# Cross attention scores as two 64-row tiles side by side, in a ring of three PSUM banks

## What is computed

```python
q, k, v = proj(query, Wq, SQ), proj(key, Wk, SKV), proj(value, Wv, SKV)   # 16 heads of 8
scores = jnp.einsum('bhqd,bhkd->bhqk', q, k) / np.sqrt(HEAD_DIM)
scores = scores + attention_bias[:, None, None, :]
probs = jax.nn.softmax(scores, axis=-1)
out = jnp.einsum('bhqk,bhkd->bhqd', probs, v)
return out.transpose(0, 2, 1, 3).reshape(B, SQ, EMBED) @ Wo.T
```

## Time and profile before

| | us |
|---|---|
| runs (median, lowest, highest) | 475.95, 474.44, 659.19 |
| the profiled execution | 473.19 |
| its span, first to last instruction | 471.4 |
| PE busy | 423.8 |
| DVE, ACT, POOL busy | 345.6, 319.2, 298.4 |

### The profile page before, as it was taken

How to read it: one execution, slowest core, us unless ns; L and a number is a source line. 1 busy time by engine, 2 the same in 40 slices (tenths; PEclk the granted TensorE clock), 3 DMA queues, 4 the chain that set the end, 5 groups by cost and what they waited for, 6 DMA issues and landing times.

```text
span 471.4 us, 16299 instructions
## 1 busy us (share of the span) xinstructions
PE 423.8 (90%) x6928; PEld 291.3 (62%) x6928; DVE 345.6 (73%) x544; ACT 319.2 (68%) x675; POOL 298.4 (63%) x250
## 2 busy tenths in 40 slices
PE   3338988988999999999999999999999899989995
PEld 2125766356676776776767767667666575555674
DVE  6363437987777877778777787778777654868796
ACT  6424632466887788788787878887877686564563
POOL 7879479689686685685775855957776461443100
PEclk9756976599999999999999999999999999999999
DMA  6476338646958858569469497495263000000000
GB/s 156 151 136 138 115 83 228 134 151 136 198 156 131 184 157 142 167 119 196 134 109 211 133 142 131 122 129 152 75 170 80 4 3 1 1 0 1 25 1 18
DMA packets 78112, 53.30 MB, mean 113 GB/s; under 512 B 62952, under 2 KB 69208, under 8 KB 78040
## 3 DMA queue, kind: packets, MB, share of 16 engines
q1 hardware_dynamic: 76216, 50.91, 48.5%
q0 software_dynamic: 1280, 0.87, 0.6%
q10 hardware_dynamic: 544, 0.48, 0.3%
HBM read 17.05 MB, written 0.46 MB: 37 GB/s over the span
## 4 chain that ended last, share of the span: by engine, by line
PE 72%; DVE 12%; ACT 5%; POOL 5%; issue 3%; DMA 2%; ACTq 1%; DVEq 0%; POOLq 0%
PE ps L1047 18%; PE ps L872 13%; PE ps L1023 6%; PE ps L375 4%; PE ps L377 4%; PE ps L376 4%; PE ps L875 4%; DVE mx L1625 3%; PE ps L1170 3%; PE ps L800 3%; PE ps L801 2%; PE ps L803 2%; DVE mself L1485 2%; PE ps L905 2%; PE ps L882 2%
## 5 line engine op out<-in xcount | busy, mean ns | idle before, releaser
L1625 DVE TENSOR_REDUCE mx<-ps 120x2 f32<-120x1000 f32 x192 | 221.2, 1195 | 55.6 <-PE ps L1023 55.6
L1319 ACT ACTIVATE p<-ps 125x448 f32<-125x448 f32 x288 | 141.6, 548 | 18.1 <-PE ps L1047 14.3
L1047 PE MATMUL ps<-qall,ks 128*125 128x224 f16 x768 | 127.0, 271 | 5.0 <-ACT p L1319 1.8
L1047 PEld LDWEIGHTS ps<-qall,ks 128*125 128x125 f16 x768 | 76.1, 137 | 43.0 <-issue 19.1
L627 POOL TENSOR_TENSOR k<-k,zero 128x500 f16<-128x500 f32 x48 | 49.8, 1038 | 69.0 <-ACT k L1249 52.7
L872 PE MATMUL ps<-p,v 125*27 125x168 f32 x1152 | 64.3, 309 | 0.0
L631 POOL TENSOR_TENSOR k<-k 128x500 f16<-128x500 f32 x48 | 54.4, 1134 | 3.8
L1319 ACT ACTIVATE wnat<-ps 125x448 f32<-125x448 f32 x96 | 47.1, 542 | 9.7 <-PE ps L1047 9.6
L613 POOL TENSOR_TENSOR ch<-ctx,ch 128x1536 f16<-128x1536 f32 x16 | 49.8, 3110 | 1.6 <-DMA ct<-ch 0.4
L1023 PE MATMUL ps<-ks,qall 31*56 31x500 f16 x768 | 44.3, 407 | 2.7 <-DVE mx L1625 2.5
L603 POOL TENSOR_TENSOR ch<-ctx,zero 128x1536 f16<-128x1536 f32 x16 | 43.9, 2747 | 2.7 <-issue 2.6
(11 more groups left out here) (198 smaller groups left out, 770.1 us busy)
## 6 DMA issues: line engine op xcount, KB each, us to landing
ks<-k SPq DMA_DIRECT2D x48, 375.0 KB
ctx<-in_ctx SPq DMA_DIRECT2D x16, 672.0 KB
ctx<-in_L_ffn_W SPq DMA_DIRECT2D x48, 64.0 KB, 2.1
ks<-brow SPq DMA_DIRECT2D x32, 46.9 KB
ctx<-in_ctx SPq DMA_DIRECT2D x16, 78.0 KB
ct<-ch SPq DMA_TRANSPOSE x32, 6.2
qall<-q POOLq DMA_DIRECT2D x12, 42.0 KB, 3.0
xs<-in_x SPq DMA_DIRECT2D x1, 448.0 KB, 4.0
```

The lines of the kernel that those rows point to most:

```text
L1047: last = mm(stb[score_bank(r, c, s, half)][0:KP, 224 * (g % 2):224 * (g % 2) + 224], ks[c % 3][:, g, KP * s:KP * s + KP], qall[:, g, :, 3 ...
L1319: A(p[s % 4][0:KP, 448 * half:448 * half + 448], stb[score_bank(r, c, s, half)][0:KP, 0:448], ACT.Exp, scale=SCALE).then_inc(exp_done, 1)
L1625: V.tensor_reduce(mx[:, h:h + 2, k // 2], mxb[0:120, 2 * pair:2 * pair + 2, 0:CH], axis=AX.X, op=ALU.max).then_inc(mx_read, 1)
```

## The change

Each score tile is made by eight matmuls in place of four: for each group one over partitions 0 to 63 (heads 0 and 1, 112 columns, into one bank) and one over partitions 64 to 127 (heads 2 and 3, 112 columns, into another bank). The row maximum on partition 127 now takes part only for heads 2 and 3; a softmax does not depend on it. Both halves of a tile signal together, when the eighth matmul is done, and ACT's exponential writes its half into `p` in four pieces of 112 columns, so that the layout of `p` stays. Score halves, small and large products now rotate through banks 0, 1 and 6 (in the last iteration also 2 and 3): `bank_table` gives each use the bank whose last use is the longest ago, and `wait_for_shared` makes the PE wait until that last use has been read. In a step the odd tile is made in one piece behind the round. In front of the loop, the DMAs of the self attention's key and query rows are shared out anew among the three queues, the first self projection waits for its own half of the input only, and the first half of the self maxima is turned one round later.

```diff
+def bank_uses():
+    order = []
+    for i in range(B):
+        for d in range(ND):
+            if d in SMALL and used(i // 3, i % 3, SMALL[d]):
+                order.append((i, SMALL[d]))
+            order += [(i, (2 * d, half)) for half in range(2)]
+            if used(i // 3, i % 3, LARGE[d]):
+                order.append((i, LARGE[d]))
+            order += [(i, (2 * d + 1, half)) for half in range(2)]
+    return order
+
+def bank_table():
+    latest, table = {bank: None for bank in SHARED_BANKS}, {}
+    for n, use in enumerate(bank_uses()):
+        if use[0] == B - 1:
+            for bank in ROUND_BANKS:
+                latest.setdefault(bank, (-1, "round"))
+        place = {u: k for k, u in enumerate(table)}
+        bank = min(latest, key=lambda k: -1 if latest[k] is None else place.get(latest[k], -1))
+        table[use] = bank, latest[bank]
+        latest[bank] = use
+    return table
+
+SHARED_BANKS, ROUND_BANKS = (0, 1, 6), (2, 3)
...
-            for row in (0, 2):
-                sp.dma_start(ks[2][row::4, :, 0:T], k12[:, 0, 0:T]).then_inc(kself_in[0], 16)
+            sp.dma_start(ks[2][0::4, :, 0:T], k12[:, 0, 0:T]).then_inc(kself_in[0], 16)
+            sp.wait_ge(q2_ok, 2)
+            query_rows(sp, 0, 0, 2, 1, qs_ok[0], (3,))
...
             query_rows(pool, 0, 0, 1, 0, qs_ok[1])
+            pool.wait_ge(kself1_ok, 2)
+            pool.wait_ge(kself2_ok, 2)
+            pool.wait_ge(kfill_ok, 1)
+            for row, part in ((1, 1), (2, 0)):
+                pool.dma_start(ks[2][row::4, :, 0:T], k12[:, part, 0:T]).then_inc(kself_in[1], 16)
             split_first(0)
...
+            def wait_for_shared(i, use):
+                if (i, use) not in BANKS or BANKS[i, use][1] is None:
+                    return
+                j, last = BANKS[i, use][1]
+                if last == "round":
+                    pe.wait_ge(mx_read, 2 * ROUNDS * B)
+                elif isinstance(last, str):
+                    pe.wait_ge(misc_read, misc_index(j // 3, j % 3, last) + 1)
+                else:
+                    pe.wait_ge(exp_done, scores_before(j // 3, j % 3) + 2 * last[0] + last[1] + 1)
...
-            pe.wait_ge(xt2_ok, 2)
             pe.wait_ge(b_loaded, 5 * 16)
             for half in range(2):
+                pe.wait_ge(xt2_ok, half + 1)
                 project(SELF_W, half, 4 + half, q_psum)
...
             for m in range(8):
                 self_round(m)
-                if m == 3:
+                if m == 4:
                     self_max_rows(0)
...
-                for half in halves:
-                    if wide(3 * r + c, s) and s % 2:
-                        pe.wait_ge(mx_read, 2 * ROUNDS * B)
-                    pe.wait_ge(exp_done, scores_before(r, c) + 2 * s + half - (3 if wide(3 * r + c, s) else 1))
-                    for g in (2 * half, 2 * half + 1):
-                        last = mm(stb[score_bank(r, c, s, half)][0:KP, 224 * (g % 2):224 * (g % 2) + 224],
-                                  ks[c % 3][:, g, KP * s:KP * s + KP],
-                                  qall[:, g, :, 3 * r + c], start=True, stop=True)
-                    last.then_inc(st_done, 1)
+                for half in range(2):
+                    wait_for_shared(i, (s, half))
+                for g in range(G):
+                    for half in range(2):
+                        rows = slice(64 * half, 64 * half + 64)
+                        last = mm(shared_bank(i, (s, half))[0:KP, 2 * S * g:2 * S * g + 2 * S],
+                                  ks[c % 3][rows, g, KP * s:KP * s + KP], qall[rows, g, 2 * half:2 * half + 2, i],
+                                  start=True, stop=True)
+                last.then_inc(st_done, 2)
...
                     large_use(r, c, LARGE[d])
-                    if live(r, c):
-                        scores(r, c, 2 * d + 1, (0,))
                     off, k = round_of(d)
                     if live(r, c + off):
                         max_round(r, c, off, k)
                     if live(r, c):
-                        scores(r, c, 2 * d + 1, (1,))
+                        scores(r, c, 2 * d + 1)
...
-            query_rows(act, 0, 0, 2, 1, qs_ok[2])
-            act.wait_ge(kself2_ok, 2)
-            act.wait_ge(kfill_ok, 1)
-            act.dma_start(ks[2][1::4, :, 0:T], k12[:, 1, 0:T]).then_inc(kself_in[1], 16)
+            query_rows(act, 0, 0, 2, 1, qs_ok[2], (0, 1, 2))
...
-                act.wait_ge(st_done, scores_before(r, c) + 2 * s + half + 1)
+                act.wait_ge(st_done, scores_before(r, c) + 2 * s + 2)
                 if half == 0:
                     act.wait_ge(pv_done, tile - 3)
-                A(p[s % 4][0:KP, 448 * half:448 * half + 448], stb[score_bank(r, c, s, half)][0:KP, 0:448], ACT.Exp, scale=SCALE
+                A(p[s % 4][0:KP].rearrange("p (g u x) -> p u g x", g=G, u=2)[:, half],
+                  shared_bank(3 * r + c, (s, half))[0:KP, 0:448].rearrange("p (g x) -> p g x", g=G), ACT.Exp, scale=SCALE
                   ).then_inc(exp_done, 1)
```

More of the change, by code:

```diff
@@ L128, in prep_index @@
     return PREP_ORDER.index((b, use)) if (b, use) in PREP_ORDER else None
-def wide(i, s):
-    return i == B - 1 or (i == B - 2 and s > KT // 2)
+def bank_uses():
[21 more added lines that the diff above has]
+SHARED_BANKS, ROUND_BANKS = (0, 1, 6), (2, 3)
+BANKS = bank_table()
 def late_index(half, use):
@@ L261, in build @@
         prep_bank, chain_bank, vbank = ps[:, 2, :], ps[:, 3, :], ps[:, 4, :]
-        stb = [ps[:, n, :] for n in range(4)]
         mxb = ps[:, 2:6, :]
@@ L407, in pick_bank @@
             return ps[:, 1, :] if s >= PAIRS else ps[:, 5, :]
-        def score_bank(r, c, s, half):
-            return half + 2 * (s % 2 if wide(3 * r + c, s) else 0)
         def late_bank(half, use):
@@ L857, in _ @@
             pe.wait_ge(qfill_ok, HG * 16)
-            for n in range(3):
-                pe.wait_ge(qs_ok[n], HG * 16)
-            pe.wait_ge(kself_in[0], 2 * 16)
-            pe.wait_ge(kself_in[1], 16)
+            for n, sent in enumerate((HG + 1, HG, HG - 1)):
+                pe.wait_ge(qs_ok[n], sent * 16)
+            pe.wait_ge(kself_in[0], 16)
+            pe.wait_ge(kself_in[1], 2 * 16)
             for m in range(8):
                 self_round(m)
-                if m == 3:
+                if m == 4:
                     self_max_rows(0)
@@ L1035, in pv_tile, with scores @@
                 times_v(v[c % 3][:, t], p[t % 4], KP, t == 0, t == KT - 1)
-            def scores(r, c, s, halves=(0, 1)):
+            def scores(r, c, s):
+                i = 3 * r + c
                 if s == 0:
                     pe.wait_ge(mrow_in[c % 3], 16 * (r + c // 3 + 1))
-                for half in halves:
-                    if wide(3 * r + c, s) and s % 2:
-                        pe.wait_ge(mx_read, 2 * ROUNDS * B)
-                    pe.wait_ge(exp_done, scores_before(r, c) + 2 * s + half - (3 if wide(3 * r + c, s) else 1))
-                    for g in (2 * half, 2 * half + 1):
-                        last = mm(stb[score_bank(r, c, s, half)][0:KP, 224 * (g % 2):224 * (g % 2) + 224],
-                                  ks[c % 3][:, g, KP * s:KP * s + KP],
-                                  qall[:, g, :, 3 * r + c], start=True, stop=True)
-                    last.then_inc(st_done, 1)
+                if i == 0 and s == 0:
+                    pe.wait_ge(exp_done, PAIRS)
+                for half in range(2):
[7 more added lines that the diff above has]
+                last.then_inc(st_done, 2)
             def large_use(r, c, use, part=None):
@@ L1324, in small_use @@
                 act.wait_ge(misc_done, misc_index(r, c, use) + 1)
+                bank = shared_bank(3 * r + c, use)
                 if use == "sel":
                     act.wait_ge(tok_ok, 3 * r + c)
-                    A(heads[:], misc[0:S, 0:144], ACT.Copy).then_inc(misc_read, 1)
+                    A(heads[:], bank[0:S, 0:144], ACT.Copy).then_inc(misc_read, 1)
                 if use == "tr":
                     first = S * (3 * r + c - 1)
-                    A(attn[:, first:first + S], misc[:, 0:S], ACT.Copy).then_inc(misc_read, 1)
+                    A(attn[:, first:first + S], bank[:, 0:S], ACT.Copy).then_inc(misc_read, 1)
                 if use == "mt":
-                    A(mrow[:], misc[0:H, 0:S], ACT.Copy, scale=1.0 / BIG).then_inc(misc_read, 1)
+                    A(mrow[:], bank[0:H, 0:S], ACT.Copy, scale=1.0 / BIG).then_inc(misc_read, 1)
             def take_heads(i):
```

27 lines of the change are left out of this document (17 added, 10 removed).

## The result

The changed kernel takes **481.1 us** (median of 20 runs, 475.5 to 483.8), the kernel before 473.4 (20 runs): ratio 1.0137, 95% interval [1.0114, 1.0159]. The forecast was 459, 450 to 471: wrong, and on the wrong side: slower, by less than the 2% that the prediction counts as a change, but clear of the noise. In this document medians are of all runs, while ratios leave out those over 1.5% above their kernel's fastest. The profiled execution took 481.02 with a span of 478.9, against 473.19 and 471.4.

A forecast was written before the change was run, and what follows sets the result against it. PE, busy throughout each 18.67 us iteration, was taken as the bound. Savings of 10.9 (iterations 1 to 12), 2.1, 0.5 and 1.7 sum to 15.2: 473.19 becomes 458.0, forecast as a median of 459, range 450 to 471.

The forecast's parts named there:

- The price of a tile: Score tile on PE: four pairs of 64-row matmuls at 0.058 us each, plus 0.05 and 0.10 for shape change: 0.38 us.
- The rival of serial loads: Score tiles: the loads of a pair go one after the other, 0.116 us a pair; slower, 494 us; chance 0.12.
- PE resumes 0.06 behind an exponential: Hand-over from ACT to PE before odd scores: PE restarts 0.06 us after the exponentials, making ACT's path 1.51 us.
- PE's own 1.52 and ACT's 1.51 tie: From even to odd scores in a step: PE's own work takes 1.52 us, the path through ACT 1.51; no slack.
- the steps of tr and mt: Two key steps whose even tile also waits for both odd exponentials: four times 1.51, 6.04 us together, 0.14 less.
- a value step: Loop step with a value projection: 2.80 us instead of 3.00, 0.20 less, three times an iteration.
- sel: Key step starting with the selection product: 0.53 + 1.51 + 1.28 = 3.32 us, 0.17 less.
- the ring's waits bind: Rival for the loop: hand-overs 0.1 us longer leave 0.1 to 0.3 gain an iteration; about the same, 468 us; chance 0.20.
- Iteration 13: Loop iteration without key projections: middle steps 8.04 us instead of 9.59, with value steps 2.1 us less, an upper end.
- Iteration 14: Late iteration hanging on DVE's rounds and the first half's norm: 0.5 us less by choice, bounds 0 and 1.5.
- Iteration 15: Last iteration: gains nothing, as ACT takes over at the same pace as PE.
- Start: In front of the loop: earlier key stack, later self maxima and input halves save 1.9 us together, 1.7 kept.

The follow-up runs named there:

- ring5_small: The changed kernel with output product read first, maxima only for heads 2 and 3, and two freed round banks added to the ring, making five: 458.1 us, ratio 0.969.
- split rounds: The kernel before with each round matmul of 500 columns cut into two of 250, 1,536 more PE instructions: 476.1 us, ratio 1.005.
- start_only: The kernel before with only the change's start (query and key rows, input halves, later self maxima): 473.5 us, ratio 1.000.

## Why the prediction was wrong

**The price of a tile was right.** The central unknown, a pair of 64-row matmuls, I took as 0.058: eight matmuls start within a tile of 0.37 (forecast 0.38), and 17.67 an iteration in ring5_small is the forecast's to 0.1 (there with five banks, so this bears out PE's own time and not the ring's). The rival of serial loads (0.116 a pair) is refuted. The rule cited with it (the Trainium skill, TensorE: Matmul & The Clock Gate, LDWEIGHTS) gives 104 ns for 125 columns; here two such loads and their matmuls take 58 ns, so as a rate it doesn't hold for loads in two row halves.

**The step that failed: "PE resumes 0.06 behind an exponential", so "PE's own 1.52 and ACT's 1.51 tie".** I read 0.06 from a single exponential at the loop's end; behind two it is 0.14, and the path is 1.60. In the steps of tr and mt, four times this path, that is 6.39 for 6.04; a value step is 2.87 for 2.80, sel 3.40 for 3.32: together the missing 0.64 of 0.91 (12 x 0.63 = 7.6 us). The rival "the ring's waits bind" had this mechanism, this condition (0.1 longer) and this result (0.1 to 0.3 left); it deserved the larger chance, since the forecast lay on a tie.

**What no step and no rival had: the supply of instructions**, 10.7 us. I counted time per instruction and never what 1,536 more instructions ask of the DMA queue that brings them. The view was there (q8, 55 packets), and one row showed DMA engines at 1.01 of their time, which I called harmless. Without the stalls the change would be at 470.4, within the range; one of the three long ones (2.7 to 3.1 each, with what it leaves) already puts it beyond. What is shown: the place in the block and in the iteration, the need for traffic and for a short block, and, with five banks, that holding the transposes back takes nearly all stalls away. What is not: why the packets at that place start later in the change than with as many instructions from split rounds, whose blocks there are about as short (6.7 to 7.2 for 6.7 to 6.9).

**Smaller terms.** Iteration 13: -2.1 expected, +1.0 found, from the wait for the output product, a ring use I had not looked for in DVE's order. Iteration 14: -0.5 expected, +0.7. Iteration 15: 0, found -0.7. Start: -1.7 expected, -0.8 in the trace, none in start_only's runs; both the moved key stack and a moved query row landed about 1 us later than forecast. 7.6 + 10.7 + 3.1 + 1.2 - 0.7 + 0.9 = 22.8, of the 23.0 between forecast and profiled execution.

## What to carry to other kernels

Where two paths tie in a forecast, the expected gain is at risk (here 0.63 of 0.91 us an iteration went): work out the hand-over from the same shape of work (two exponentials, not one), and look for slack in banks before making the engine faster. When a change adds instructions to an engine that is 90% busy, count its instruction packets and look where DMA bursts overlap them; idle time put down to issue in the middle of a tile, at equal distances in the instruction count, may be an engine without instructions. Then ask what the change has made needless: here half of the maxima, whose banks were what the ring lacked.

## What the runs showed of the hardware

An instruction packet that comes late stops PE even with PE 90% busy: 1.3 to 1.6 us a time in the three long stalls of the change, and 1.4 to 1.6 more behind each, in which the granted clock is at half for a time (1.2 GHz for 2.4). The Trainium skill, Runtime: NRT & Kernel Launch, Instruction fetch mechanics, tells of 256 instructions to a block of 16 KiB, which agrees with the packets' size and the distance of the stalls. It also calls the fetch hidden behind the pace of issue; in this kernel it was not.

Four round matmuls in two row strips take 0.33 where eight in four take 0.34; each strip carries two of them in both. And transposes cost the DMA engines more beside a context load than behind it: 0.81 against 0.62 of an iteration.
